# The first image's expert inputs made in the last turn of the second attention; two orders of work changed

## Time and profile before

| | us |
|---|---|
| median of three runs | 1869.66 (1868.59 to 1869.83) |
| the profiled execution | 1862.18, its span 1860.4 |
| PE busy in the span | 1757.0 (94%) |
| DVE busy | 1007.1 (54%) |
| ACT busy | 674.2 (36%) |
| POOL busy | 407.2 (22%) |
| mean granted clock | 0.982 |

### The profile page before, as it was taken

The page is one execution under the profiler, slowest core; times in us unless marked ns, Lnnn a source line. Parts: engine busy times, 40 slices in busy tenths (PEclk is TensorE's granted clock), DMA queues, the critical chain, the costliest instruction groups (busy, mean ns, idle before and its releaser), DMA issues. The chain is left out here.

```text
span 1860.4 us, 29106 instructions
## 1 busy us (share of the span) xinstructions
PE 1757.0 (94%) x9935; PEld 1118.6 (60%) x9935; DVE 1007.1 (54%) x2072; ACT 674.2 (36%) x1289; POOL 407.2 (22%) x415
## 2 busy tenths in 40 slices
PE   7989999899999987899989999997999999999997
PEld 3324444344444433677755656655676768999997
DVE  6597877778777877788874554442311111122221
ACT  2116655556566675455432332223111110111110
POOL 2101021120211001788831212110121211100100
PEclk9989999999999999999999999998999999999999
DMA  6832632525425111000056000000010003343311
GB/s 198 132 54 65 91 78 40 99 53 84 78 40 93 25 48 56 17 0 0 1 198 195 1 0 0 0 0 1 18 37 23 30 24 102 124 151 102 105 32 33
DMA packets 111955, 112.84 MB, mean 61 GB/s; under 512 B 11455, under 2 KB 104433, under 8 KB 111858
## 3 DMA queue, kind: packets, MB, share of 16 engines
q1 hardware_dynamic: 98610, 83.21, 20.1%
q10 hardware_dynamic: 9600, 18.92, 2.9%
q0 software_dynamic: 3648, 9.46, 1.4%
HBM read 78.51 MB, written 32.93 MB: 60 GB/s over the span
## 5 line engine op out<-in xcount | busy, mean ns | idle before, releaser
L925 DVE TENSOR_REDUCE mx<-ps_a 128x1 f32<-128x384 f32 x768 | 383.2, 550 | 66.3 <-PE ps_a L567 63.8
L789 ACT ACTIVATE prob<-ps_a 128x768 f32<-128x768 f32 (+1 forms) x512 | 306.2, 650 | 118.7 <-PE ps_a L580 118.6
L567 PE MATMUL ps_a<-w,qs 96*128 96x384 bf16 x768 | 220.1, 338 | 12.3 <-DVE mx L925 5.2
L580 PE MATMUL ps_a<-qs,w 100*128 100x384 bf16 x768 | 208.8, 332 | 6.1 <-issue 3.4
L2090 PEld LDWEIGHTS ps_e<-xTr,w 128*128 128x128 f32 x1792 | 206.1, 193 | 2.2 <-issue 0.8
L2090 PE MATMUL ps_e<-xTr,w 128*128 128x128 f32 x1792 | 206.3, 276 | 0.6 <-DVE xTr L2263 0.6
L567 PEld LDWEIGHTS ps_a<-w,qs 96*128 96x128 bf16 x768 | 61.4, 98 | 180.8 <-DVE mx L925 116.6
L2026 PE MATMUL ps_e<-xT_all,w 128*128 (+1 forms) x512 | 169.3, 490 | 0.9 <-ACT xT_all L2117 0.9
L591 PE MATMUL ps_a<-prob,vp 128*32 128x384 f32 x1536 | 164.1, 500 | 0.0
L2026 PEld LDWEIGHTS ps_e<-xT_all,w 128*128 128x128 f32 x512 | 97.4, 192 | 66.2 <-issue 1.4
L2153 ACT ACTIVATE gel_r<-ps_e 128x512 f32<-128x512 f32 x56 | 33.4, 597 | 280.9 <-PE ps_e L2090 280.9
(11 more groups left out here) (253 smaller groups left out, 2490.2 us busy)
## 6 DMA issues: line engine op xcount, KB each, us to landing
w<-parts_dram SPq DMA_DIRECT2D x192, 96.0 KB, 5.3
w<-in_L_ffn_W_dram ACTq DMA_DIRECT2D x18, 1024.0 KB, 8.3
parts_dram<-w SPq DMA_DIRECT2D x24, 576.0 KB, 3.4
qs<-parts_dram SPq DMA_DIRECT2D x96, 96.0 KB, 4.0
prob<-in_x_dram SPq DMA_DIRECT2D x24, 256.0 KB, 3.6
w<-in_L_ffn_W_dram SPq DMA_DIRECT2D x6, 1024.0 KB, 12.6
grouped_x<-empty_row SPq DMA_DIRECT2D x1, 4352.0 KB, 23.7
grouped_h<-empty_row SPq DMA_DIRECT2D x1, 4240.5 KB, 33.1
```

What stands on the lines that cost most here:

```text
L567: mm = pe.matmul(ps[:, r % 3, 0:T], qs[0:NS, b, u // 2, t * P:(t + 1) * P], ks[0:NS, b, u % 2, u // 2], start=True, stop=True)
L580: mm = pe.matmul(ps[:, 4 + t, 0:T], ks[0:NS + 4, b, kp, hh, t * P:(t + 1) * P], qs[0:NS + 4, b, hh], start=True, stop=True)
L789: act.activation(prob[:, g % 2, j, ts.start:ts.stop], ps[:, 4 + ts.start:4 + ts.stop, 0:T], ACT.Exp).then_inc(exp_done.sem, 1)
L925: dve.tensor_reduce(at, ps[:, r % 3, 0:T], AX.X, ALU.max).then_inc(ring_free.sem, 1)
```

## The change

Three edits, in their order in time.

- First attention: the second maxima product of a unit is issued before the products with the values instead of after them.
- End of the feed-forward: DVE does `scaled(1)` before the second group of moments instead of after it, and PE does `down(B - 1, 2)` before it waits for sc_copied.
- Last turn of the second attention: DVE turns the moments of 21 tiles (all but the last image's) into mean and variance and normalises image 0 into a new buffer x0; ACT takes the square root; PE turns x0 into PSUM banks 0 and 1 after its gathering products; ACT copies it to a new buffer xT0 between its two groups of copies. The experts stage then handles only the last three tiles' moments at its start, and PE begins with `gate_up(0, 0)` on xT0. Six semaphores and 6 KB of SBUF per partition are added.

```diff
                         scores(i, b, v, 1)
+                        if more:
+                            ring(i + 1, 1 - b, ring_part(v)[1:2])
                         if j and g:
                             values(i, b, g - 1, j - 1)
...
                         if more:
-                            ring(i + 1, 1 - b, ring_part(v)[1:])
+                            ring(i + 1, 1 - b, ring_part(v)[2:])
...
+                def expert_inputs():
+
+                    dve.wait_ge(stats_done.sem, stats_done.at(B - 1, 0))
+                    for n in range(KNOWN):
+                        dve.bn_aggr(mv[:, n], bn[:, n]).then_inc(entry_aggr.sem, 1)
+                    dve.wait_ge(entry_root.sem, 1)
+                    dve.reciprocal(rstd[:, 0:KNOWN], rstd[:, 0:KNOWN]).then_inc(entry_rstd.sem, 1)
+                    dve.wait_ge(entry_rstd.sem, 1)
+                    for t in range(TT):
+                        dve.tensor_scalar(E["x0"][:, t], h[:, t], mv[:, t, 0:1], rstd[:, t:t + 1],
+                                          ALU.subtract, ALU.mult).then_inc(entry_xn.sem, 1)
+
                 def turn1(i, b, more):
                     if more:
                         inputs1(i + 1, 1 - b)
+                    else:
+                        expert_inputs()
...
                 add(B - 1, 1)
+                scaled(1)
                 stats(EARLY_ROOTS + 6, EARLY_ROOTS + 12)
                 new_moments(EARLY_ROOTS, EARLY_ROOTS + 12)
-                scaled(1)
...
-                for n in range(NT):
+                for n in range(KNOWN, NT):
                     dve.bn_aggr(mv[:, n], bn[:, n]).then_inc(aggr_done.sem, 1)
...
+                def turn_expert_inputs():
+                    pe.wait_ge(sub_done.sem, sub_done.at(B, 0))
+                    pe.wait_ge(entry_xn.sem, TT)
+                    for k in range(KC):
+                        for t in range(TT):
+                            mm = pe.transpose(ps[:, k, t * P:(t + 1) * P], E["x0"][:, t, k * P:(k + 1) * P], ident[:])
+                    mm.then_inc(entry_xt.sem, 1)
...
                     if more:
                         scores(i + 1, 0, 0)
+                    else:
+                        turn_expert_inputs()
...
                 turn_hidden(B - 1, 2)
+                down(B - 1, 2)
                 pe.wait_ge(sc_copied.sem, 2)
-                down(B - 1, 2)
...
                     if more:
                         copy_inputs1(i + 1)
+                    else:
+                        act.wait_ge(entry_aggr.sem, KNOWN)
+                        act.activation(rstd[:, 0:KNOWN], mv[:, 0:KNOWN, 1], ACT.Sqrt, bias=G["eps"][:]
+                                       ).then_inc(entry_root.sem, 1)
...
                     if more:
                         exps(i + 1, 0)
+                    if not more:
+                        act.wait_ge(entry_xt.sem, 1)
+                        act.copy(E["xT0"][:], ps[:, 0:2, 0:T]).then_inc(entry_xT.sem, 1)
                     copy_attn(i, 4, PAIRS)
...
-                turn_inputs(0)
-                pe.wait_ge(xT_done.sem, 1)
+                pe.sem_inc(xt_done.sem, 1)
                 for a in range(IT1):
                     gate_up(0, a)
...
-                act.activation(rstd[:], mv[:, :, 1], ACT.Sqrt, bias=G["eps"][:]).then_inc(root_done.sem, 1)
-                copy_inputs(0)
+                act.activation(rstd[:, NT - TT:], mv[:, NT - TT:, 1], ACT.Sqrt, bias=G["eps"][:]).then_inc(root_done.sem, 1)
+                act.sem_inc(xT_done.sem, 1)
...
+                dve.sem_inc(xn_done.sem, TT)
+                inputs(1)
                 dve.wait_ge(root_done.sem, 1)
-                dve.reciprocal(rstd[:], rstd[:]).then_inc(rstd_done.sem, 1)
+                dve.reciprocal(rstd[:, NT - TT:], rstd[:, NT - TT:]).then_inc(rstd_done.sem, 1)
                 dve.wait_ge(rstd_done.sem, 1)
-                inputs(0)
-                inputs(1)
```

More of the change, by code:

```diff
@@ L1249, in middle @@
         stats_done, aggr_done = sig("stats_a1", TT), sig("aggr_a1")
+        entry_aggr, entry_root, entry_rstd = sig("entry_aggr"), sig("entry_root"), sig("entry_rstd")
+        entry_xn, entry_xt, entry_xT = sig("entry_xn"), sig("entry_xt"), sig("entry_xT")
+        KNOWN = (B - 1) * TT
         empty_done, expert_w_in, empty_in = sig("empty_done"), sig("expert_w_in"), sig("empty_in")
@@ L1489, in _ @@
                 dve.wait_ge(stats_done.sem, stats_done.at(B, 0))
-                for n in range(NT):
+                for n in range(KNOWN, NT):
                     dve.bn_aggr(mv[:, n], bn[:, n]).then_inc(aggr_done.sem, 1)
-                dve.wait_ge(aggr_done.sem, NT)
+                dve.wait_ge(aggr_done.sem, NT - KNOWN)
             @block.gpsimd
@@ L1843, in _ @@
                 for_pairs(act, turn1)
+                act.wait_ge(entry_xT.sem, 1)
 E8 = 8
@@ L1863, in expert_buffers @@
             "w3": ctx.enter_context(nc.sbuf_tensor("w3", [P, 3, IT1, C], F32)),
+            "x0": ctx.enter_context(nc.sbuf_tensor("x_entry", [P, TT, C], F32)),
+            "xT0": ctx.enter_context(nc.sbuf_tensor("xT_entry", [P, KC, T], F32)),
             "empty": ctx.enter_context(nc.sbuf_tensor("empty_row", [P, C + 1], F32)),
@@ L1935, in experts, with x_of, xT_of @@
         w_in = [sig(f"w_in{e}") for e in range(E8)]
+        def x_of(n):
+            return E["x0"][:, n] if n < TT else xall[:, n]
+        def xT_of(i):
+            return E["xT0"][:] if isinstance(i, int) and i == 0 else xT_all[:, i]
         def first_slots(eng):
@@ L1984, in move_x @@
                         pool.indirect_dma_start(xs_dram, bass.IndirectOffsetOnAxis(ap=pos_i[:, n:n + 1], axis=0),
-                                                xall[:, n], None).then_inc(x_placed.sem, 16)
+                                                x_of(n), None).then_inc(x_placed.sem, 16)
                 def move_h(i):
@@ L2018, in turn_inputs @@
                         for t in range(TT):
-                            mm = pe.transpose(ps[:, 6 + k, t * P:(t + 1) * P], xall[:, i * TT + t, k * P:(k + 1) * P], ident[:])
+                            mm = pe.transpose(ps[:, 6 + k, t * P:(t + 1) * P], x_of(i * TT + t)[:, k * P:(k + 1) * P], ident[:])
                     mm.then_inc(xt_done.sem, 1)
@@ L2026, in gate_up @@
                             mm = pe.matmul(ps[:, 2 * (a % 2) + m, 0:T], w12[:, 0, m, k, a * P:(a + 1) * P],
-                                           xT_all[:, i, k], start=(k == 0), stop=(k == KC - 1))
+                                           xT_of(i)[:, k], start=(k == 0), stop=(k == KC - 1))
                     mm.then_inc(gu_done.sem, 1)
@@ L2051, in _ @@
                         for j in range(LANES):
-                            mm = pe.matmul(ps[j * LANE:(j + 1) * LANE, g, 0:T], wg[:, k], xT_all[:, g * LANES + j, k],
+                            mm = pe.matmul(ps[j * LANE:(j + 1) * LANE, g, 0:T], wg[:, k], xT_of(g * LANES + j)[:, k],
                                            start=(k == 0), stop=(k == KC - 1), tile_position=(0, j * LANE))
```

## The result

| | before | after |
|---|---|---|
| median of 5 runs (lowest to highest), us | 1868.59 (1862.48 to 1869.83) | 1851.33 (1849.57 to 1851.69) |
| profiled execution, us | 1862.18 | 1851.40 |
| its span, us | 1860.4 | 1849.6 |
| PE busy | 94% | 1758.3 us, 95% |
| granted clock, mean | 0.982 | 0.982 |

The ratio is 0.9911, with an interval of 0.9897 to 0.9926: faster by 0.9%, clear of noise, 17.3 us between the medians. A second set of runs of the same two kernels on another occasion gave 1866.19 (11 runs) and 1849.90 (6 runs), ratio 0.992 (0.9903 to 0.9936), 16.3 us. The forecast was 1855.1 in 1851.0 to 1861.0.

What follows compares the result with a forecast made beforehand. PE, busy 94% of the span, was taken as the bound, so only its idle or lower-clock time counts. Gains 5.0 + 2.9 + 6.7 = 14.6 us off the 1869.66 median gave 1855.1, range 1851.0 to 1861.0.

Steps and rivals of the forecast that it cites:

- Part 1: First attention: one maxima product ahead of the values shortens waits, 3.8 + 2.9 - 1.7 = 5.0 us gained.
- the base: Whole kernel: the forecast gain is subtracted from the median 1869.66, not from the profiled 1862.18, the difference being unexplained.
- The sign that was named: First attention: the forecast is wrong if its 577 us do not shorten by about 5.
- Part 2: End of the feed-forward: down starts 1.21 us earlier and the clock staying up gives 1.7, sum 2.9.
- 0.88 will be left: Before down: of 2.09 us of PE idleness 0.88 remains, so the clock is taken to stay up.
- Part 3: Experts' entry: first product 6.6 us earlier, 1.76 of old clock loss regained, 1.6 charged for the lower clock; sum 6.7.
- I charged 1.6: Experts' start: after 3.4 us of idleness the lower clock is assumed for the first 3 us, costing 1.6.
- covers in the last turn: Second attention's last turn: idle times hide the added DVE, PE and ACT work; a lost one costs at most 0.7 or 0.8 us.
- rival 1: Experts' start: the clock does not fall behind the shorter gap, so the entry gives 8.4 us; 1853.4, chance 0.12.
- 2: First attention: the early maxima product gains nothing, since the transposition waits as long; total gain 9.6, 1860.1 us, chance 0.14.
- rival 3: First attention: the early maxima product holds the values in every unit having them, losing 23.5 us; 1883.6, chance 0.04.
- 4: Experts' entry: PE's first product waits for something overlooked, gaining 4 instead of 6.7 us; 1857.8, chance 0.08.

Runs made afterwards that it cites:

- after_again: The changed kernel, unchanged, run and profiled once more beside the follow-up runs; 1849.90 us (6 runs), ratio 0.992 to the kernel before.
- part 1 alone: Kernel before, with only the second maxima product of a unit issued ahead of the values; 1857.24 us, ratio 0.9949.
- e4: Changed kernel, with five useless products after the last output product to fill the idle gap before the experts; 1847.30 us, ratio 0.9896.
- e7: Changed kernel, with five useless products filling the gap before the experts and two maxima products ahead of the values in unit 31; 1844.51 us, ratio 0.988.
- e8: Changed kernel, with all maxima products of every unit ahead of the values; 1869.32 us, ratio 1.0018 to the kernel before.
- e6: Changed kernel, with two maxima products ahead of the values in units 15 and 31; 1847.69 us (one run).
- part 2 alone: Kernel before, with only scaled(1) ahead of the moments and down(B - 1, 2) ahead of its wait; 1863.82 us, ratio 0.9991.
- part 3 alone: Kernel before, with only the experts' entry changed, its first inputs prepared in the last turn; 1858.32 us, ratio 0.9957.
- before_again: The kernel before, unchanged, profiled once more for its spread; 1868.91 us.

## Why the prediction was right

**The sum.** Forecast 14.6, medians 17.3 and 16.3. Worked out again from the traces it is 7.6 + 2.9 + 5.3 to 6.7 = 15.8 to 17.2 (after_again has 7.1 in the seven turns), so the excess is in part 1. The mechanisms were right; the time, 1851.33, lies only 0.3 above the low end of the range. Of the 3.8 us between it and 1855.1 the gain accounts for 2.7 and the base for 1.1 (1869.66 over three runs, 1868.59 over five). The sign that was named, the first attention about 5 us shorter, is met by 5.2, and that is partly luck: the seven turns gave 7.6 and the eighth took 2.4 back by its clock.

**Part 1, 5.0 forecast, 7.6 measured.** Mis-sized are the count and, more, the clock, which had no term. The sizes per unit were right: 31 gave 0.30 (0.30), 15 gave 0.26 (0.24), 24 and 28 gave 0.23 (0.21), 1 and 23 cost 0.14 and 0.13 (0.14). But not every turn pays in unit 1: four do, the second, third, fifth and sixth (in the sixth the cost stands behind a larger gain of the clock). The first turn pays in neither unit and gains 0.23 in two more, 8 and 20; the last one gains it in unit 12. Some 0.07 a turn is lost in small pieces elsewhere. So the order gives 5.8, not 5.0. The other 1.8 is clock, which the prediction did not have at all. At the start of the sixth turn, before and after:

```profile
517.90:530.00 12.10, 11.75 (x68) 5.78 (x68) 8.67 (x21) 6.44 (x11) 0.00 (x0) 0.86 0.63 95
```

```profile
514.80:530.00 15.20, 14.57 (x95) 7.03 (x99) 11.87 (x28) 9.18 (x16) 0.59 (x1) 1.00 0.74 108
```

The lower clock stood there in all four traces with the old order and in none of the seven with the new one (part 1 alone, e4 to e7, both of the whole change), nor in e8. It is worth about 1.1, since the sixth turn gained 1.77 where the fifth gained 0.66; a second such place, at the start of the fourth turn, was halved, from 6.8 us to 3.4, in five of the seven (not in e6 and e7), and gave 0.7. The gain came with the order in the single-part run too, so it belongs to part 1. Why the clock no longer falls there was not settled. In the four old traces the low stretch begins 1.2 to 1.3 us into the sixth turn. With the new order that turn also begins some 4 to 6 us sooner after the first score product, so whether the waits inside the turns keep the clock up, or only the other moment at which the turn begins, no run separates.

**Part 2, 2.9 forecast, 2.9 measured** (-1.2 to the start of `down`, -1.7 in it and behind). "0.88 will be left" was 0.89, and the clock stayed up behind it, in the whole change and in part 2 alone. What the prediction took for granted, that 2.09 us of idleness cost the clock, was so in three of four traces; in the fourth part 2 would have given 1.2.

**Part 3, 6.7 forecast, 5.3 to 6.7 measured.** PE's first product came 6.67 nearer to the last output product (6.6 forecast). The clock fell, as I had taken it. I charged 1.6 for it. From an idle start the eight records take 2.82 at full clock (e4, e7), so 4.31 and 4.51 cost 1.5 and 1.7, and the 5.46 of the first profile 2.6. By the same measure the lower clock before (4.34) cost 1.5, not 1.76. None of the covers in the last turn gave way.

One row under this choice was read wrongly. The prediction took the stretch 712.00 to 734.30, at 1.00 with PE mostly idle, as a sign that a gap can go unpunished. The window ends just where the clock falls:

```profile
734.30:737.70 3.40, 2.99 (x5) 1.85 (x6) 2.86 (x9) 1.12 (x3) 0.14 (x1) 0.50 0.26 55
```

In all twelve traces PE's first products of the feed-forward, behind 4.34 to 4.38 us of idleness, meet the lower clock. So this row spoke for the choice that was made, and not for rival 1. That one and the same gap may or may not cost the clock is shown by the 2.09 before `down` instead.

The Trainium skill, "ScalarE: Activation LUTs", section "What ACT_TABLE_LOAD costs", prices a switch of table at 1283 ns and about 1380 ns of drain. The trace of the kernel before has the 1.28 and not the second term: the root follows its load (1278.67 and 1.28) at once.

```profile
1279.96 0.31 ACT L2131 ACTIVATE rstd<-mv,eps 128x24 f32<-128x24 f32 x1
```

In the kernel after there is no second load behind the barrier: the root's table is loaded in the last turn and stays until the gelu. ACT's load ended at 1274.16 and its gelu then waited 4.07 for PE's products, so by the page nothing would have been late here either.

The Trainium skill, "TensorE: Matmul & The Clock Gate", Part 1, says that the gate is free-running and does not start anew with the kernel, so that one kernel shows a different number of products at the lower clock from run to run. The runs agree: behind 3.36 or 3.37 of idleness the eight records took 4.31 in one trace, 4.51 in three and 5.46 in two.

**The rivals.** 1 (the clock does not fall) did not happen by itself, and happened when the gap was filled: it was worth 1.7 to 2.6 there, where 1.6 had been charged. 2 (no gain from the ring) is excluded by part 1 alone. 3 did not happen with one product ahead. With all of them ahead, in e8, its mechanism is there, and the seven turns are 14.0 us longer than before where rival 3 charged 23.5. 4 is excluded by part 3 alone.

**The base.** Carrying the forecast gain over to the median, and not to the profile, was right. The difference of the first two profiles, 10.8, is 4 short of the forecast, since a short execution of the old kernel stands against one of the new in which the eighth turn and the experts' entry met the lower clock; before_again and after_again differ by 21.1, the other way. The medians lie between.

**Open.** Which stretches at 1.2 GHz the single timed runs had (only profiled ones show their clock); why the sixth turn keeps its clock with the new order; the small waits of e8 in units where DVE seemed to have room.

## What to carry to other kernels

An issue order of a saturated engine can be changed for nothing as long as the moved instruction's buffer is free by then: move it by one, read the spacing at which the consumer frees the buffers (0.47 here), and stop when the next one has to wait. Where a barrier leaves the tensor engine idle, put the first stage's inputs ahead of it in other engines' idle time, and then fill the rest of the gap with products: the lower clock behind 3.4 us of it cost 1.5 to 2.6 us more. Compare profiles by unit and wait, never by span, when the clock alone moves an execution by 7 us.

## What the runs showed of the hardware

- The kernel's spread of 7 to 9 us between runs is, where two profiles could be compared, time at 1.2 GHz: 86 us against 67 us, for an execution 6.7 us longer; the seven turns in both agree to 0.2 us.
- Idleness of PE and the granted clock behind it, at four places: 4.34 to 4.38 before the feed-forward, 0.50 in twelve traces of twelve; 3.36 or 3.37 before the experts, 0.50 in six of six, for 6.8 us in two and for 3.4 in four; 2.09 before `down`, 0.50 in three of four; 1.33 (fill) and 0.89 (`down`), 1.00 in two of two and eight of eight.
- It was enough to fill 2.0 of the 3.37 us: behind the 1.33 that were left the records ran at full clock.
- One more operation in DVE's queue (a projection's remainder, 0.56 us) was enough to take the whole gain of a second product ahead in unit 15: the gain is 0 in the six turns that have it and 0.45 in the one that has not.
